# Words of source tiles shared: GpSimd makes five of the thirteen, by a comparison and a product, ahead of the gathers of last edges

## The reference, cut to what matters

```python
for t in range(num_rounds):
    msg_in = jnp.concatenate([hv[dst], hv[src], e], axis=1)
    msgs = msg_in @ W_msg[t] + b_msg[t]
    a = jax.ops.segment_sum(msgs, dst, num_segments=num_nodes)
    hv = _gru_cell(a, hv, ...)
...
agg = jax.ops.segment_sum(x_j, col, num_segments=N)          # third layer
out = mean @ W_l + b_l + x @ W_r
out = out + jnp.zeros_like(out).at[col].set(e)               # the last edge of each node wins
```

## Time and profile before

| what | value |
|---|---|
| median of 3 runs | 4950.62 us (4948.92 to 4953.69) |
| the profiled execution | 4948.67 us, of which the span of the trace is 4946.6 us |
| PE busy | 3317.7 us, 67% of the span |
| PEld busy | 2513.4 us, 51% |
| DVE busy | 2832.9 us, 57% |
| ACT busy | 886.4 us, 18% |
| POOL busy | 2097.5 us, 42% |
| line 1857 (the 13 source words) | 35.4 us of DVE |

### The profile page before, as it was taken

The page is one execution under the profiler, slowest core; times in us unless marked ns, Lnnn a source line. Parts: engine busy times, 40 slices in busy tenths (PEclk is TensorE's granted clock), DMA queues, the critical chain, the costliest instruction groups (busy, mean ns, idle before and its releaser), DMA issues. The chain is left out here.

```text
span 4946.6 us, 93310 instructions
## 1 busy us (share of the span) xinstructions
PE 3317.7 (67%) x24444; PEld 2513.4 (51%) x24445; DVE 2832.9 (57%) x7446; ACT 886.4 (18%) x1811; POOL 2097.5 (42%) x2644
## 2 busy tenths in 40 slices
PE   2333277777769889899989744555555666666666
PEld 1222123333329889798989633334444444444445
DVE  6555788777765544311323355555566666666775
ACT  1111113566650022200001100000000000000002
POOL 4666700000000021111111277777777777777770
PEclk6555699888889999999999755555555555555558
DMA  3000000111125424354544322223222333333330
GB/s 141 0 0 0 4 14 33 52 58 58 58 92 172 150 71 159 123 174 156 189 153 158 91 64 64 66 67 70 69 69 71 74 72 75 74 76 73 77 77 19
DMA packets 173539, 403.74 MB, mean 82 GB/s; under 512 B 47902, under 2 KB 109481, under 8 KB 172809
## 3 DMA queue, kind: packets, MB, share of 16 engines
q1 hardware_dynamic: 52409, 259.35, 14.7%
q10 hardware_dynamic: 69360, 91.59, 6.6%
q0 software_dynamic: 51680, 51.82, 6.0%
HBM read 359.52 MB, written 43.07 MB: 81 GB/s over the span
## 5 line engine op out<-in xcount | busy, mean ns | idle before, releaser
L697 POOL DMA_INDIRECT scr<-ptable,src_i x1566 | 1522.1, 972 | 481.6 <-issue 398.3
L666 POOL COPY late<-late 128x256 f32<-128x256 f32 (+1 forms) x65 | 25.8, 398 | 1949.6 <-POOLq L664 1949.6
L1030 PE MATMUL ps_front<-scr,arena 128*128 128x192 bf16 x7203 | 612.2, 248 | 67.2 <-PEq L1028 67.2
L1139 PE MATMUL ps_front<-stat_w,scr 128*128 128x392 fp8e4 x2064 | 494.2, 370 | 239.4 <-PEq L1143 214.3
L1030 PEld LDWEIGHTS ps_front<-scr,arena 128*128 128x128 fp8e4 x7203 | 601.0, 98 | 76.9 <-issue 74.9
L900 ACT ACTIVATE arena<-arena 128x384 f32<-128x384 f32 x309 | 161.6, 523 | 1859.9 <-ACTq L899 1859.9
L952 PE MATMUL ps_front<-arena 128*128 (+1 forms) x930 | 176.7, 363 | 434.3 <-PEq L950 434.3
L1651 DVE TENSOR_TENSOR scr<-scr,late 128x384 bf16<-128x384 f16 x1024 | 360.5, 352 | 183.7 <-DVEq L1650 176.4
L1139 PEld LDWEIGHTS ps_front<-stat_w,scr 128*128 128x128 bf16 x2064 | 187.8, 105 | 507.8 <-issue 467.0
L952 PE MATMUL ps_back<-arena 128*128 x924 | 175.5, 363 | 402.0 <-PEq L950 402.0
L1030 PE MATMUL ps_front<-arena 128*128 128x192 bf16 x4802 | 406.4, 248 | 23.1 <-PEq L1028 23.1
(11 more groups left out here) (342 smaller groups left out, 5043.5 us busy)
## 6 DMA issues: line engine op xcount, KB each, us to landing
arena<-a_dram SPq DMA_DIRECT2D x245, 784.0 KB, 4.3
arena<-low_dram ACTq DMA_DIRECT2D x309, 192.0 KB, 3.3
a_dram<-arena SPq DMA_DIRECT2D x49, 784.0 KB, 3.3
arena<-in_e32g ACTq DMA_DIRECT2D x309, 96.0 KB, 3.3
scr<-ptable,src_i POOLq DMA_INDIRECT x1566
arena<-in_e16p SPq DMA_DIRECT2D x1, 13387.5 KB, 35.3
x<-in_x_nm SPq DMA_DIRECT2D x1, 1664.0 KB, 8.2
out_nm<-x SPq DMA_DIRECT2D x1, 1664.0 KB
```

The lines of the kernel that those rows point to most:

```text
L697: pool.indirect_dma_start(grow[:, g % RING, j, :], None, ptable, bass.IndirectOffsetOnAxis(ap=src_i[:, g * GC + j:g * GC + j + 1], axis=0) ...
L1030: last = pe.matmul(ps_z[b % 2][:, 0:3 * H], amat[b][:, i, :], hsp[k % 2][:, i, :], start=(i == 0), stop=(i == NT - 1))
L1139: return pe.matmul(bank_w[i][:, 0:WC], oh_lo[u][:, j, :], oh_hi[u][:, j, :], **{"start": False, "stop": False, **flags})
```

## The change

GpSimd makes words 8 to 12 of `src_words`, DVE makes words 0 to 7 (`WV = 8`). GpSimd has no fused form here: it writes the comparison of `srch` with k (five `tensor_scalar`), waits for them, and then multiplies the five words by the byte number (five `tensor_tensor`), which it reads as an integer copy `src_int`. For this DVE works out `src_byte` and `srch` first, copies `src_byte` to `src_int` (one added instruction) and signals `s_srcs`; the operations on `dst` come behind. DVE waits for GpSimd's words (`s_srcw`) behind its own eight, ahead of the window table. `src_byte` moves to another buffer, `srch` no longer shares its place with the low bits of `src` (they get `src_low`), and two operations are 1568 columns wide instead of 1664. On GpSimd the ten operations stand between the last `residues` and the gathers.

```diff
-        src_byte = late[:, CHP:CHP + CHB]
+        src_byte = stat_w[:, 0:CHB]
...
+        WV = 8
+        src_int = scr[:, lo_at:lo_at + CHB].bitcast(i32)
+        src_low = scr[:, NT * F16:NT * F16 + CHB].bitcast(i32)
...
             all_visits(pool, 5, 6, residues)
 
+            pool.wait_ge(s_srcs, 1)
+            pool.sem_inc(s_srcs, -1)
+            for k in range(WV, NTQ):
+                last = pool.tensor_scalar(src_words[:, :, k], srch[:, 0:CHB], float(k), None, ALU.is_equal)
+            last.then_inc(s_pool, 1)
+            pool.wait_ge(s_pool, 1)
+            pool.sem_inc(s_pool, -1)
+            for k in range(WV, NTQ):
+                last = pool.tensor_tensor(src_words[:, :, k], src_words[:, :, k], src_int, ALU.mult)
+            last.then_inc(s_srcw, 1)
             pool.wait_ge(s_last, 1)
...
-            v.tensor_scalar(dsub, dst_i, 3, 26, ALU.bitwise_and, ALU.logical_shift_left)
...
-            v.tensor_scalar(srch, src_i[:, :], P - 1, None, ALU.bitwise_and)
...
-            link(v.tensor_tensor(lokey, lokey, srch, ALU.add))
             link(v.tensor_scalar(src_byte.bitcast(i32), src_i[:, 0:CHB], 7, 3, ALU.logical_shift_right, ALU.bitwise_and))
             v.tensor_scalar(srch, src_i[:, :], 9, None, ALU.logical_shift_right)
...
             link(v.tensor_scalar(src_byte, src_byte, 1.0 / 32, None, ALU.mult))
+            v.tensor_copy(src_int, src_byte).then_inc(s_srcs, 1)
+            v.tensor_scalar(dsub, dst_i, 3, 26, ALU.bitwise_and, ALU.logical_shift_left)
...
+            v.tensor_scalar(src_low, src_i[:, 0:CHB], P - 1, None, ALU.bitwise_and)
...
+            link(v.tensor_tensor(lokey[:, 0:CHB], lokey[:, 0:CHB], src_low, ALU.add))
...
-            for k in range(NTQ):
+            for k in range(WV):
                 last = v.scalar_tensor_tensor(out=src_words[:, :, k], in0=srch[:, 0:CHB], scalar=float(k), in1=src_byte,
                                               op0=ALU.is_equal, op1=ALU.mult)
             link(last)
+            v.wait_ge(s_srcw, 1)
+            v.sem_inc(s_srcw, -1)
```

More of the change, by code:

```diff
@@ L319, in gnn @@
         s_cum = sem("s_cum")
+        s_srcs = sem("s_srcs")
+        s_srcw = sem("s_srcw")
         s_ones = sem("s_ones")
@@ L1838, in _ @@
             v.sem_inc(s_last, 1)
-            v.tensor_scalar(dsub, dst_i, 3, 26, ALU.bitwise_and, ALU.logical_shift_left)
-            link(v.tensor_scalar(dsel, dst_i[:, 0:CHB], 2, 1, ALU.logical_shift_right, ALU.bitwise_and))
-            link(v.tensor_scalar(dsub, dsub, ONES_F, None, ALU.bitwise_or))
-            link(v.tensor_tensor(dst_word[:, :, 1], dsub_f[:, 0:CHB], dsel, ALU.mult))
-            v.tensor_scalar(srch, src_i[:, :], P - 1, None, ALU.bitwise_and)
-            link(v.tensor_tensor(dst_word[:, :, 0], dsub_f[:, 0:CHB], dst_word[:, :, 1], ALU.subtract))
-            link(v.tensor_scalar(dsub, dst_i, 3, None, ALU.logical_shift_right))
-            link(v.tensor_scalar(lokey, dsub, float(P), None, ALU.mult))
-            link(v.tensor_tensor(lokey, lokey, srch, ALU.add))
             link(v.tensor_scalar(src_byte.bitcast(i32), src_i[:, 0:CHB], 7, 3, ALU.logical_shift_right, ALU.bitwise_and))
@@ L1853, in _ @@
             link(v.tensor_scalar(src_byte, src_byte, 1.0 / 32, None, ALU.mult))
+            v.tensor_copy(src_int, src_byte).then_inc(s_srcs, 1)
+            v.tensor_scalar(dsub, dst_i, 3, 26, ALU.bitwise_and, ALU.logical_shift_left)
+            link(v.tensor_scalar(dsel, dst_i[:, 0:CHB], 2, 1, ALU.logical_shift_right, ALU.bitwise_and))
+            link(v.tensor_scalar(dsub, dsub, ONES_F, None, ALU.bitwise_or))
+            link(v.tensor_tensor(dst_word[:, :, 1], dsub_f[:, 0:CHB], dsel, ALU.mult))
+            v.tensor_scalar(src_low, src_i[:, 0:CHB], P - 1, None, ALU.bitwise_and)
+            link(v.tensor_tensor(dst_word[:, :, 0], dsub_f[:, 0:CHB], dst_word[:, :, 1], ALU.subtract))
+            link(v.tensor_scalar(dsub, dst_i, 3, None, ALU.logical_shift_right))
+            link(v.tensor_scalar(lokey, dsub, float(P), None, ALU.mult))
+            link(v.tensor_tensor(lokey[:, 0:CHB], lokey[:, 0:CHB], src_low, ALU.add))
             for w in range(WT):
                 v.tensor_scalar(iota_w[:, w, :, :].rearrange("p s a -> p (s a)"), iota_h[:, 0:P], float(w * P), None, ALU.add)
-            for k in range(NTQ):
+            for k in range(WV):
                 last = v.scalar_tensor_tensor(out=src_words[:, :, k], in0=srch[:, 0:CHB], scalar=float(k), in1=src_byte,
```

## The result

| | before | after |
|---|---|---|
| median of 5 runs | 4950.86 us (4948.92 to 4953.69) | 4971.85 us (4969.61 to 4976.13) |
| ratio | | 1.0043, 95% interval [1.0028, 1.0057] |
| profiled execution, its span | 4948.67, 4946.6 us | 4969.61, 4967.8 us |
| DVE busy | 2832.9 us | 2862.9 us |
| POOL busy | 2097.5 us | 2125.1 us |

The changed kernel is slower by 21 us, 0.4%. The forecast was 4966, with 4955 to 4984 as the range.

A forecast was written before the change was run, and what follows sets the result against it. The prediction took DVE's path before the build as the bound: 31.5 us of GpSimd work, less 3 of overlap, less 12.8 saved on DVE, plus 0.3 for the signal, gives +16 and 4966 us; range 4955 to 4984.

The forecast's parts named there:

- The bound of the stage: Before the build, DVE alone sets the end: a microsond on it between 517.49 and 572.4 us moves everything behind by as much.
- DVE's own path, 12.8 us shorter: DVE before the build: five fewer words save 13.6 us, the cast costs 0.9, narrower operations give back 0.15.
- The two streams take turns: Before the build, DVE and GpSimd wait for each other, so the end is the sum of both: +16 us net.
- Rival A: Before the build, both engines run side by side and the full 12.8 us are gained: 4937.8 us; chance 0.08.
- Rival D: Before the build, GpSimd starts only when DVE is done: +19 us, 4969.6; counted within the forecast's chance of 0.67.
- Rival B: Turns are taken, but GpSimd's ten operations cost only 23.5 to 25.4 us: about 4959 us; chance 0.17.
- GpSimd's price: The ten GpSimd operations before the gathers: 2.2 us a comparison, 4.1 a product, 31.5 us together.
- the high end: GpSimd's ten operations with a stride factor of 1.6: 2.5 us a comparison, 5.1 a product, 38 us together.
- The overlap at a change of turn: Where DVE and GpSimd alternate before the build, about 0.3 us hidden for each of ten operations: 3 us off.
- The stage in sum: Preparation before the build ends 16 us later, with bounds of +7 and +23.5 within the mechanism of turns.
- rival C: GpSimd has a slow form for integer operands or comparisons, 55 to 60 us for the ten: about 4992 us; chance 0.08.
- The gathers: GpSimd's gathers start near 588 us instead of 518.37 at no cost, with more than 1000 us of cover.

The follow-up runs named there:

- e8: All 13 words on DVE in the changed kernel's order without the cast, eleven of them made twice as a pure delay: ratio 1.0061 to the kernel before.
- e2: The changed kernel, but DVE waits for GpSimd's five words right behind the cast, so the two never work at once there: ratio 1.0074 to the kernel before.
- e3: DVE makes all 13 words; before that GpSimd's ten operations, then five extra DVE words, write neighbouring columns as scratch: 5689.47 us, before 5648.06 on that chip.
- e4: DVE makes all 13 words; GpSimd only writes, 28 memsets of 1568 columns into a free buffer beside DVE: 5671.93 us, before 5648.06 on that chip.
- e11: The kernel with early keys and paired words, plus one GpSimd comparison and one product of one integer column: 4933.23 us, ratio 0.9960 to the kernel before.
- e6: All words on DVE, build signalled ahead of them so ACT's keys start early, two neighbouring words per instruction: 4938.74 us, ratio 0.9970 to the kernel before.
- e9: The kernel before plus one GpSimd comparison of one integer column behind the last residues: 4952.53 us, ratio 0.9998.
- e10: The kernel before plus one GpSimd product of one integer column behind the last residues: 4951.98 us, ratio 1.0000.
- e12: The kernel with early keys and paired words, plus two GpSimd comparisons of one integer column: 4931.82 us, ratio 0.9973 to the kernel before.

## Why the prediction was right, and what was off

- **The bound of the stage** was read rightly: DVE's path from 517 us to the window table, and all behind it moves with it. e8 shows it, 29 to 30 us for 31.
- **DVE's own path, 12.8 us shorter.** Right as far as it can be taken apart: e2, where nothing overlaps, has 101.6 us of preparation, and 64.9 - 12.8 + 48.9 + 0.3 is 101.3.
- **The two streams take turns.** Right in the main, with 42 of 49 us not hidden, and it decided the sign. Rival A (side by side) would have had the window table near 560; it starts at 602.15. Rival D (DVE always wins) is wrong too: from 524.60 on the eight DVE operations let one of GpSimd's each go first, and GpSimd was done before the first word. Rival B (GpSimd near 23.5 us) is out by the 48.9 of e2.
- **GpSimd's price.** This is the term that was mis-sized: 31.5 us forecast, 48.9 measured. The product was right (4.1 forecast, 4.27 measured; the estimate of 4.8 beside it was too high, as the step adds 0.79 to 3.48 and not half as much again). The comparison was put at 2.2 us and took 5.45 (e2), beyond the high end of 2.5. Its low end came from a cast of one input, which does not compare. Of the 3.25 us that were missing, 2.6 are the comparison itself, which takes 4.16 us with neighbouring columns (e3); 1.3 are its strided output, of which the forecast had already 0.7.
- **The overlap at a change of turn.** Forecast 3 us for ten, measured 7.0 (e2 against the changed kernel). The prediction took 0.3 for each of ten turns. The turns beside a `tensor_scalar` were near that (0.2 to 0.5), but two sums went almost whole beside comparisons, 1.6 us each; the rows of 256 columns that the 0.3 came from have no such pair.
- **The stage in sum:** +16 forecast, +29.7 measured: 17.4 more of GpSimd, 4 less by the turns. This lies beyond the +23.5 that the prediction gave as the bound within its mechanism.
- **What was not in the forecast at all:** the 9.3 us that the last stage is shorter. Two misses of opposite sign, 14 us too few for the stage and 9 too many for the rest, leave the median 6 us from the forecast (4971.85 against 4966). That the number is so near is luck. The range would have held without the 9.3 us as well (about 4981), but only because it went beyond the mechanism's own bound of 4974, some way towards rival C.
- **The gathers** cost nothing by starting later, as said; the build's stage is alike in both kernels (866.0 and 865.2 us). The cover was overstated: DVE asks for them at the end of the one-hots, at 1447 us in the kernel before and at 1477 in the changed one, not at 1690. There it is 817 us behind the last gather, not more than 1000.
- **Rival C** (a slow form on GpSimd for comparisons) had a chance of 0.08 and the right idea: the comparison is slow, the product is not, and the ten take 49 us rather than 55 to 60. The sign that the prediction named for it, comparisons with a pitch above 4 us where DVE is away, is what e2 shows: 5.5 us from one start to the next.

## What to carry to other kernels

Work moved from DVE to GpSimd that reads SBUF was for the most part not parallel work here, beside DVE's `tensor_scalar`s and operations with two SBUF inputs: 42 of its 49 us were added to DVE's path, at GpSimd's price, and the words of this kernel cost 9.7 us there for 2.7 us saved. Before an operation is moved off an engine, look at why it is slow where it is: here an output step of 52 bytes cost DVE 1.1 us a word, and writing two neighbours at once took 9.6 us off the stage where the transfer to GpSimd added 30. And where a time agrees with a forecast, compare the stages as well: two errors can cancel.

## What the runs showed of the hardware that was not expected

- GpSimd's comparison of 1568 integer columns takes 4.16 us, longer than the product of two inputs at 3.48; both with neighbouring columns (e3).
- GpSimd's memsets run beside DVE's words at full pace (1.40 us), but its gathers do not: at 580.19 in the changed kernel one took 11.53 us, and in the earlier trace rows one took 21.45. In e4 the first gather behind the memsets took 13.82 us, until the words were through. So a gather can be held up under a DVE operation with two SBUF inputs, by which part of it no run here shows.
- Two of DVE's sums of 1.79 us ended 0.2 us behind the GpSimd comparison beside them and did not lengthen the next one; the sum beside a GpSimd product ended 1.6 us behind it (changed kernel, lines 1864, 1866 and 1869).
- One integer comparison and one integer product on GpSimd, of a single column each, are enough to bring the median of 1566 later gathers from 952 to 944 ns (e11 against e6, e9, e10, e12).
